# First attention: the shift of two consecutive score steps in one pass of four 32-row tiles that opens both steps' accumulation

## The reference, cut to what matters

```python
q = ln_lat @ Wq
kv = jnp.concatenate([xn, ln_lat], axis=1) @ Wkv
k, v = jnp.split(kv, 2, axis=-1)          # 16 heads of 64
weight = jnp.einsum('bhld,bhnd->bhln', q * scale, k * scale)
weight = jnp.where(full_mask[:, None, None, :], weight, neg)
weight = jax.nn.softmax(weight, axis=-1)
out = jnp.einsum('bhln,bhnd->bhld', weight, v)
return out @ Wout
```

## Time and profile before

| | before |
|---|---|
| median of 3 executions | 3516.6 us |
| lowest and highest | 3516.3 and 3516.61 us |
| profiled execution | 3512.97 us |
| its span, first to last instruction | 3511.0 us |
| TensorE matmul busy | 3116.8 us, 89% of the span |
| VectorE, GpSimd, ScalarE busy | 2454.7, 2095.5, 1738.7 us |

### The profile page before, as it was taken

One profiled execution on the slowest core, in us unless ns is written; L12 is line 12 of the kernel. 1 busy time (PEld: TensorE's weight loads), 2 busy tenths in 40 slices (PEclk: granted clock), 3 DMA queues, 4 the chain that ended last, 5 costly groups with the idle time before them and its releaser, 6 DMA issues. The chain is left out here.

```text
span 3511.0 us, 56665 instructions
## 1 busy us (share of the span) xinstructions
PE 3116.8 (89%) x23380; PEld 1187.8 (34%) x23380; DVE 2454.7 (70%) x2971; ACT 1738.7 (50%) x1811; POOL 2095.5 (60%) x985
## 2 busy tenths in 40 slices
PE   3599999999999999999999999995863799999947
PEld 1233433333333333343343333332541233333224
DVE  5567677777677667767777767754564687888748
ACT  3144444444444444444444444452430587877833
POOL 0087898788888888789788888896110221211022
PEclk7799999999999999999999999997875799999969
DMA  1000000000000000000000000001000100000000
GB/s 57 0 6 1 1 7 1 1 7 1 1 1 7 1 1 7 1 1 7 1 1 3 1 1 1 1 1 45 1 20 13 54 9 17 9 11 8 2 1 25
DMA packets 29296, 29.19 MB, mean 8 GB/s; under 512 B 9517, under 2 KB 26606, under 8 KB 29038
## 3 DMA queue, kind: packets, MB, share of 16 engines
q1 hardware_dynamic: 29038, 25.57, 2.4%
HBM read 17.68 MB, written 2.10 MB: 6 GB/s over the span
## 5 line engine op out<-in xcount | busy, mean ns | idle before, releaser
L410 POOL TENSOR_TENSOR a_acc_p<-a_acc_p,a_prob 128x1024 f32<-128x1024 f32 x704 | 1718.1, 2440 | 355.4 <-ACT a_prob L468 283.6
L468 ACT ACTIVATE a_prob<-slot,a_mask_bias 128x1024 f32<-128x1024 f32 x928 | 989.8, 1111 | 926.1 <-PE slot L685 925.3
L502 DVE TENSOR_REDUCE a_part_max<-wide 128x2 f32<-128x1024 f32 x896 | 1091.3, 1218 | 493.4 <-PE wide L666 485.2
L700 PE MATMUL bank<-a_prob,a_val 128*64 128x512 f32 x3712 | 895.5, 604 | 0.2 <-ACT a_prob L468 0.2
L1075 ACT ACTIVATE a_prob<-slot,a_mask_bias 128x1024 f32<-128x1024 f32 x416 | 455.4, 1116 | 80.9 <-PE slot L1261 70.4
L666 PE MATMUL wide<-a_k_hi,a_q_hi 64*128 64x512 f16 (+1 forms) x2048 | 359.6, 363 | 63.2 <-DVE a_part_max L502 58.3
L1125 DVE TENSOR_REDUCE a_part_max<-wide 128x1 f32<-128x512 f32 x514 | 334.5, 683 | 90.7 <-PE wide L1249 54.5
L700 PEld LDWEIGHTS bank<-a_prob,a_val 128*64 128x64 f32 x3712 | 226.4, 136 | 434.9 <-issue 320.9
L685 PE MATMUL slot<-a_q_hi,a_k_hi 64*128 64x512 f16 x1856 | 353.1, 377 | 9.0 <-DVE a_k_lo L493 4.8
L685 PE MATMUL slot<-a_q_lo,a_k_hi 64*128 64x512 f16 x1856 | 352.6, 377 | 0.0
L685 PE MATMUL slot<-a_q_hi,a_k_lo 64*128 64x512 f16 x1856 | 352.4, 376 | 0.0
(11 more groups left out here) (295 smaller groups left out, 3271.5 us busy)
## 6 DMA issues: line engine op xcount, KB each, us to landing
a_w_staged<-in_w SPq DMA_DIRECT2D x8, 384.0 KB, 3.1
x_res<-in_x SPq DMA_DIRECT2D x1, 2048.0 KB, 8.7
a_q_op<-a_hi SPq DMA_DIRECT2D x128, 16.0 KB, 1.8
out_x<-x_res SPq DMA_DIRECT2D x16, 128.0 KB, 1.7
nx_context<-in_ctxt SPq DMA_DIRECT2D x1, 1601.0 KB, 6.5
a_w_staged<-in_w1a SPq DMA_DIRECT2D x4, 385.0 KB, 3.1
ctx_rows<-in_ctx SPq DMA_DIRECT2D x1, 1536.0 KB
a_k_op<-a_hi SPq DMA_DIRECT2D x96, 16.0 KB, 1.8
```

Source lines behind the costliest of these rows:

```text
L410: nc.gpsimd.tensor_tensor(acc, before, prob[:, k % R, :], ALU.add).then_inc(added_p, 1)
L468: nc.scalar.activation(prob[:, k % R, :], slot[:, :], ACT.Exp, bias=mbias[:, t:t + 1]).then_inc(probs_ready, 1)
L502: nc.vector.reduce_max(part_max[:, w % 2, :, j, c], pairs, AX.X).then_inc(max_used, 1)
L700: ins = nc.tensor.matmul(av[r, :], val[g % 2][:, t, r], prob[:, k % R, h * QB:(h + 1) * QB], start=(t == 0), stop=(t == NT - 1), tile_posi ...
```

## The change

The fourth term moves out of `scores` into a new function `lower(w, ts)`, which stands before `pair` of every even step and serves that step and the following odd one. It issues four matmuls with 32 contracted rows each, in the four 32-row tiles of the array; they write the two halves of the two slots and open their accumulations (`start=True`). The three other terms follow in `scores` and no longer open one. For step 28, which has no partner, `lower` issues two matmuls. Where the slots of both steps have to be free before anything is written, both calls of `free_slot` now stand at the beginning of `lower`, and `scores` has none.

So that the shift lies in all four groups of 32 partitions, `neg_max` is laid out as 2 copies by 2 heads by 32, `max_of` writes it with two reductions where there was one, the counts of `neg_ready` are doubled, and `pick` is made by a reduction over the identity.

```diff
+        self.row = 32
...
-        neg_max = sb("neg_max", [P, 2, HALF])
+        neg_max = sb("neg_max", [P, 2, 2, a.row])
...
-                nc.vector.tensor_reduce(neg_max[:, :, 0:a.blocks], part_max[:, w % 2, :, :, :], AX.X, ALU.max, negate=True).then_inc(neg_ready, 1)
+                for copy in range(2):
+                    nc.vector.tensor_reduce(neg_max[:, copy, :, 0:a.blocks], part_max[:, w % 2, :, :, :], AX.X, ALU.max, negate=True).then_inc(neg_ready, 1)
...
-            nc.vector.tensor_tensor(pick[:, :], m.ident[:, 0:a.blocks], m.ident[:, HALF:HALF + a.blocks], ALU.add)
+            rows = m.ident[:, :].rearrange("p (n c) -> p c n", c=a.row)[:, 0:a.blocks, :]
+            nc.vector.reduce_max(pick[:, :], rows, AX.X)
...
+            def lower(w, ts):
+                if ts[0] == 0:
+                    pe.wait_ge(shift_ready, w + 1)
+                for t in ts:
+                    free_slot(("scores", w, t))
+                for i, t in reversed(list(enumerate(ts))):
+                    for h in range(2):
+                        r0 = (2 * i + h) * a.row
+                        r = slice(r0, r0 + a.row)
+                        nc.tensor.matmul(half(("scores", w, t), h), ones16[r, :], shift[w % 2][r, :, :].rearrange("p j q -> p (j q)"),
+                                         start=True, stop=False, tile_position=(r0, 0))
+
             def scores(w, t):
...
-                free_slot(what)
-                if t == 0:
-                    if u == 0:
-                        pe.wait_ge(lo_done, kq(g, a.nkq - 1))
-                    pe.wait_ge(shift_ready, w + 1)
+                if t == 0 and u == 0:
+                    pe.wait_ge(lo_done, kq(g, a.nkq - 1))
...
-                terms = [(kh[p], qh[p]), (kh[p], ql[p]), (kl[p], qh[p]), (None, None)]
+                terms = [(kh[p], qh[p]), (kh[p], ql[p]), (kl[p], qh[p])]
...
                     if t % 2 == 0:
+                        lower(w, range(t, min(t + 2, NT)))
                         if n < S:
                             pair(n)
                         scores(w, t)
```

More of the change, by code:

```diff
@@ L420, in _ @@
             split(0)
-            nc.gpsimd.memset(neg_max[:, :, :], 0.0)
+            nc.gpsimd.memset(neg_max[:, :, :, :], 0.0)
             nc.gpsimd.memset(ones16[:, :], 1.0)
@@ L498, in pair @@
                 if i == 0 and w >= 2:
-                    dve.wait_ge(neg_ready, w - 1)
+                    dve.wait_ge(neg_ready, 2 * (w - 1))
                 if i < NT - 1:
@@ L682, in scores @@
                         r = slice(h * HALF, (h + 1) * HALF)
-                        left = ones16[r, :] if k is None else k[r, ks]
-                        right = shift[w % 2][r, :, :].rearrange("p j q -> p (j q)") if q is None else q[r, qs]
-                        ins = nc.tensor.matmul(half(what, h), left, right, start=(n == 0), stop=(n == len(terms) - 1),
+                        ins = nc.tensor.matmul(half(what, h), k[r, ks], q[r, qs], start=False, stop=(n == len(terms) - 1),
                                                tile_position=(h * HALF, 0))
@@ L725, in turn @@
             def turn(w):
-                pe.wait_ge(neg_ready, w + 1)
+                pe.wait_ge(neg_ready, 2 * (w + 1))
                 if w >= 2:
                     pe.wait_ge(res_added, 2 * (w - 1))
-                nc.tensor.transpose(side[:, 0:P], neg_max[:, :, :].rearrange("p h c -> p (h c)"), m.ident[:, :]).then_inc(turned, 1)
+                nc.tensor.transpose(side[:, 0:P], neg_max[:, :, :, :].rearrange("p k h c -> p (k h c)"), m.ident[:, :]).then_inc(turned, 1)
             place = {what: n for n, what in enumerate(order)}
```

## The result

| | before | changed |
|---|---|---|
| median of 4 executions each | 3516.45 us | 3646.43 us |
| lowest and highest | 3512.28 and 3516.61 | 3641.79 and 3648.14 |
| ratio, with its 95% interval | | 1.0371 (1.0353 to 1.0388) |
| profiled execution | 3512.97 | 3645.79 |
| its span | 3511.0 | 3644.0 |

The changed kernel is 130 us slower; the forecast was 109 us slower. In the profiled executions the last `sums` of the first attention starts at 2422.28 us before and at 2549.25 after, so 127 us arise there. The rest of the program, whose code is the same, took 1088.7 us before (3511.0 - 2422.28) and 1094.75 after. Those last 6 us are no effect of the change that can be told apart: in the twelve profiled executions of this record this same part took between 1083.3 and 1098.2 us. Of the 6 us, 4.4 are longer waits of TensorE for the loads of `a_q_op` (69.6 us after, 65.2 before).

A forecast was written before the change was run, and what follows sets the result against it. TensorE sets the pace, with VectorE's reduction a floor between `pair`s. Terms 17.5 + 6 - 3 + 28.5 + 37.4 + 23.5 = +110 us on 3512.97 give 3623, 3626.6 for the median, said as 3625; range 3578 to 3665.

The forecast's parts named there:

- The floor: Between the two `pair`s of two steps: VectorE's reduction keeps them at least 1.71 us apart.
- The new pass: `lower` ahead of the first `pair`: costs 0.33 us, bounds 0.22 and 0.55, with 0.10 for the shape change.
- rival C: In `lower`, the four row tiles run in two pairs, 0.43 + 0.12 us, giving 3694; chance 9%.
- D: At `lower`'s shape change: the forecast without the drain, 3588 us and a little around it, 3570 to 3600; chance 14%.
- The estimate of 0.28 us for the pass: For the four-tile pass in `lower`: 4 x 0.217 / 3.07 = 0.28 us, from a documentation page's 3.07 times.
- The moved waits: Before `lower`: +0.92 us at unit ends (31), +0.89 behind query or key projections (42), +0.84 behind value projections (28).
- The late steps: Steps 10, 18, 20, 26: late `pair` swallows `lower`, nothing; VectorE's lost air in steps 12 to 18 adds 6 us.
- A: Second `pair` not held by the reduction, moved waits covered: removed passes count in full, 97 us, 3420; chance 4%.
- B: Over the first attention, gain and waits cancel, -97 + 101 = +4, about 3520 us; needs A's floor; chance 3%.

The follow-up runs named there:

- the kernel with late waits and the shared maximum: Changed kernel with 64-row terms at unit ends and behind projections, and ScalarE copying half of `wide` in even steps for VectorE's maximum: 3457.14 us, ratio 0.9837.

## Why the prediction was right

*The bound.* TensorE sets the pace. But between the two `pair`s of two steps, the reduction on VectorE sets it as soon as two passes are gone from there. The floor was read as 1.71 and is 1.72. Half a reduction took it away in the changed kernel and did nothing to ordinary steps before: shown.

*The new pass.* Put at 0.33, bounds 0.22 and 0.55; it is 0.32 to 0.33. The two-tile `lower` shows that four tiles cost no more than two, so rival C, four tiles in two pairs, is out. The gap of 0.10 between `pair` and a `lower` behind it shows that a change of shape costs time, and with it D, no drain, is out. The split of `lower` into 0.22 and 0.10 is inferred from these. The estimate of 0.28 us for the pass, which the prediction sets beside its sum, does not fit it.

*The moved waits.* Forecast as 0.92, 0.89 and 0.84 us, measured 1.04, 1.01 and 0.90. The terms were mis-sized by the signal: 0.05 was taken from a `pair` with one wait in front of it, but `lower` has two or three and starts 0.15 behind the last. With one wait it is 0.05. That is 9 of the 21 us by which the forecast fell short.

*The late steps.* Steps 10, 18, 20 and 26 were put at nothing, and 0.2 us was given for VectorE having less room from step 12 to 18. They are 0.37 a unit, half of it step 10. This is the sum's second mis-sized term, 5.5 us. The forecast took one instance of step 18 for all four: step 18 does cost next to nothing (0.02), the others don't.

*The rest.* 6 us lie in the part of the program that was not changed, within what that part scatters by.

*What was to be seen.* Right: 0.33 from `lower` to `pair`, 4.2 us for two steps, idling of 1.5, 0.8 and 1.3 us in front of `lower`, no work added on ScalarE and GpSimd, the clock unchanged (0.99), and GpSimd still deciding the end of the last unit (TensorE waits 13.5 us for it, before 13.3). What was not right: that TensorE's idling in front of `pair` would grow by 30 us. It fell, from 61.9 over the whole program to 58.0, because a gap of 0.2 us disappears under the modelled end of the matmul before it. The distance between two starts showed it, the idle column did not.

*Rivals A and B.* A needed a floor under 1.52 and covered waits. Neither held. The kernel with late waits and the shared maximum shows that the condition at the floor was rightly named: with it met, the pass does pay. But it pays about 0.10 us in two steps and not the 0.217 that A counts, since the shape change still takes 0.10.

## What to carry to other kernels

A pass saved on the busiest engine is worth what the narrowest distance around it allows: measure the distance between two dependent starts, and compare it with what the other engine needs, before counting the pass. When two steps are opened by one instruction, their waits are merged too, and everything queued behind the earlier one stops being cover. Here that alone cost about 90 us, nearly the 97 that rival A gave the pass.

## What the runs showed of the hardware

- A `lower` with two or three waits in front of it started 0.15 us behind the last of what it waited for (102 places, 0.143 to 0.147); with one wait, 0.05 to 0.06 at the same 102. The number of waits is not all of it: in the run that only moved the waits, where `pair` adds its own wait for the reduction, it was 0.10 behind projections and 0.25 at unit ends. What decides was not tried.
- Four 32-row tiles took as long as two, to 0.01 us. The way from 64 rows to 32 cost 0.10 us, and so did the way from 32 to 64, if the pass of 32-row tiles takes the 0.22 of one of 64-row tiles.
- From the values to the next pass it was 1.87 us, whether that was a `pair` with 64-row tiles (before) or a `lower` with 32-row tiles (changed).
- With shorter reductions VectorE's additions of 128x1024 took longer, 2.92 us on the mean in the changed kernel against 2.38 (the group of 96), and 2.72 against 2.36 in the kernel before. Why was not tried.
